# A message-passing layer on one core: fewer and differently placed loads around SyncE's queue

## The chip, the cores and the metric

The kernel runs on one core of a Trainium2 chip. The metric is the device time of one execution in microseconds (us); less is better. The median of three runs before the change is 9704.65 us (9703.06 to 9709.19).

## The reference, cut to what matters

12,500 nodes have 32 features each (8 scalars and 8 vectors of 3). 412,500 edges, sorted by receiver, have ten features (`emb`), a direction and a weight. Two small networks turn the ten features into 512 and 384 weights for each edge; with them the features of sender and receiver are multiplied, gated by a tanh, and added up at the receiver.

```python
xs, xd = x[edge_src], x[edge_dst]
s1 = concat([xs[:, :8], xd[:, :8]]); v1 = concat([xs[:, 8:].reshape(E, 8, 3), xd[:, 8:].reshape(E, 8, 3)])
w = relu(emb @ fc1_w1 / sqrt(10)) @ fc1_w2 / 4          # 512 weights of each edge
vdot1 = einsum('euk,ek->eu', v1, sh1) / SQRT3
s_t = a1 * (einsum('eu,euw->ew', s1, Wss) + einsum('eu,euw->ew', vdot1, Wvv))
v_t = a1 * (einsum('eu,euw->ew', s1, Wsv)[:, :, None] * sh1[:, None, :] + einsum('euk,euw->ewk', v1, Wvs))
# w2: 384 weights in the same way; scal, gates, vecs from s_t and v_t
edge_out = concat([tanh(scal), (vecs * tanh(gates)[:, :, None]).reshape(E, 24)]) * norm[:, None]
x = layernorm(x + segment_sum(edge_out, edge_dst, num_segments=12500))
```

## The kernel before, in words

Edges are worked on in tiles of 128 and in periods of eight tiles (1024 edges), 403 periods in all. float32 factors of matmuls are split into three bf16 pieces, which stand one below the other in six groups of rows. The work of one period is spread over five passes of a loop (`body`); in a pass each engine runs a fixed list of steps, each for the period whose turn it is. Seen from a pass `at`, the names are: `four_on`, `three_on`, `zero`, `one`, `two`, `three`, `four` for the periods at+4, at+3, at+2, at+1, at, at-1 and at-2. Between engines only semaphores set the order; each engine's list is written out by hand. Two passes stand in one turn of the loop, since buffers alternate by parity (`par`). There are passes -2 to 404; the first four and the last few stand outside the loop.

**SyncE** issues all direct loads and stores. In a pass it issues, in this order: `load_emb` for at+4 (the ten features); `load_indices` for at+3 (the senders' indices, half of a record, from `rec`); `load_late_base` for at-1 (the receivers' first node, for VectorE's window of sums); `load_near` for at+1 (for each of eight tiles it reads the tile's first receiver from `near_base` into a register and loads eight nodes' rows of `t_rows` from there); `load_near_bases` for at+3; `turn_hid(one, 0)` (a transposing DMA of `hid_parts` for layer 0, without which TensorE's `fill(one, 0)` can't start); `load_late` for `two` (the receivers' offsets, the other half of the record); `stack_emb` for at+3 (six copies of ten rows each, `emb_parts` to `emb_stack`); `stack_off`; `turn_hid(one, 1)`; and in every second pass `store_nodes` (a table piece of 256 KB to `t_rows`, and the load of `xt`).

**GpSimd** issues eight indirect gathers of node rows per pass (`gathers`, line 855), with small elementwise steps between them: `messages_scalar` needs the tanh, `hid_less_first` and `hid_less_second` make the last pieces of `hid_parts`, `emb_less_second` those of `emb_parts`.

**ScalarE** copies sums out of PSUM and applies the tanh. In a pass: `scalar_sums_back`, `emb_first`, `out_sums_out` (`osum_t`, line 1065), `node_scalars` (`prods`, line 1038), `tanh_out` (`th`, line 1070), `hidden_out`, `row_scalars`, `row_vectors`, `emb_second`, `hidden_first`, `vector_sums_out`, `near_hidden` 0, `hidden_second`, `off_hots` (eight squares), `near_hidden` 1, `scalar_sums_out`, `nodes_made`, `one_hot`, `gate_sums_out`.

**TensorE** makes each edge's weights with `fill` (line 1350, five kinds in two alternating buffers `pw`), VectorE multiplies them with the features, and TensorE adds the products by transposing them into one sum (`added`, line 1355). In a pass it ends with `nodes_made` (line 1254), `fill(one, 0)` and `gate_sums`; the next begins with `fill(two, 1)`, `out_sums`, `receivers` (line 1337, needs the receiver loads), `hidden` (line 1300, needs `emb_stack`), `four_sums_turned` (before the tanh).

**VectorE** waits for the tanh in `q_first` (`along`, line 1775), in the middle of its list; in `program` it also reads the window's first node from `late_base` into a register (line 1890).

The parts that the change touches:

Of the kernel before, what the change touches and what calls it, by code (L numbers as in the profile page):

```python
# [5 lines left out]
P = 128  # L6
G = 8
SUPER = P * G
WINDOW = 42
NEAR = 8  # L10
C = 8
F = 32
H = 16
L1, L2 = 256, 384
PIECES = 6
# [21 lines left out]
def build_gnn_layer(nc, x, src, dst, emb_t, vec, weight, fc1_w1, fc1_w2, fc2_w1, fc2_w2, out):  # L37
# [34 lines left out]

    def in_pieces(tile, dram, full, width, lo, hi, last):
# [37 lines left out]
    with ExitStack() as ctx:  # L111
# [10 lines left out]
        same_period = sb("same_period", [P, P])  # L122
# [29 lines left out]
        idx = sb("idx", [P, 2, G], I32)  # L152
        idx_dst = sb("idx_dst", [P, 2, G], I32)
        near_base = sb("near_base", [1, 2, G], I32)
# [4 lines left out]
        late_off = sb("late_off", [P, 2, G], I32)  # L159
        late_base = sb("late_base", [1, 2, G], I32)  # L160
# [28 lines left out]
        var = sb("var", [P, NB])  # L189
# [13 lines left out]

        UNIT = G * C
# [121 lines left out]
        idx_in = [sem(f"idx_in{i}") for i in range(2)]  # L326
# [10 lines left out]
        stack_in = [sem(f"stack_in{i}") for i in range(2)]  # L337
        late_in = [sem(f"late_in{i}") for i in range(2)]
        late_base_in = [sem(f"late_base_in{i}") for i in range(2)]
# [16 lines left out]
        begun = sem("begun")  # L356

# [156 lines left out]

        block = ctx.enter_context(nc.Block())
# [3 lines left out]
        def _(sp):  # L519
# [8 lines left out]
            def stack_emb(a, is_general=True):  # L528

                p = a.par  # L530
                if not is_general:
                    wait(sp, near_mm, a.before(2).n(2, 2))
                sp.wait_ge(emb_c, a.n(1, 1))
                wait(sp, hid_mm, a.before(2).n(1, 1))
# [25 lines left out]
            def load_indices(a, is_general):  # L560

                p, s, two = a.par, a.index(), a.before(2)
                wait(sp, nodes_in[p], two.k(16 * G))
                sp.dma_start(idx[:, p, :], rec[:, s, 0:G]).then_inc(idx_in[p], 16)  # L564
                if is_general:
                    wait(sp, t_edges_in, two.n(16 * G, 16 * G))
                    sp.sem_inc(begun, 1)
                    sp.dma_start(idx_dst[:, p, :], last_tiles if a.is_last() else dst_tiles[s],
                                 allow_slow_non_contiguous=True).then_inc(idx_dst_in[p], 16)

            def load_near_bases(a):
                p = a.par
                sp.dma_start(near_base[:, p, :], base_rows[:, bass.ds(a.index() * G, G)]).then_inc(near_base_in[p], 16)  # L573

            def load_near(a):
# [8 lines left out]
                for t in range(G):  # L584
                    first = nc.sync.value_load(near_base[0:1, p, t:t + 1], min_val=0, max_val=N - 1)  # L585
                    sp.dma_start(t_near[:, p, t, :], t_rows[bass.ds(first * H, NEAR * H), :]).then_inc(t_near_in[p], 16)  # L586
# [11 lines left out]
            def load_late(a, is_general):  # L598
                p, s, two = a.par, a.index(), a.before(2)
                if is_general:  # L600
                    wait(sp, rel_done, two.n(1, 1))
                    sp.dma_start(late_off[:, p, :], last_tiles if a.is_last() else dst_tiles[s],
                                 allow_slow_non_contiguous=True).then_inc(late_in[p], 16)
                else:
                    wait(sp, off_hot_done, two.n(G, G))
                    sp.dma_start(late_off[:, p, :], rec[:, s, G:2 * G]).then_inc(late_in[p], 16)  # L606
# [1374 lines left out]
```

## Time and profile before

| | us |
|---|---|
| median of the runs shown | 9704.65 |
| the profiled execution's own time | 9652.08 |
| its span, on which all rows are | 9650.3 |
| TensorE matmuls busy | 6180.1 (64%) |
| VectorE busy | 4712.0 (49%) |
| GpSimd busy | 4658.2 (48%) |
| ScalarE busy | 3364.6 (35%) |

The mean granted TensorE clock is 0.788 of full speed. SyncE has no busy time of its own in the profile; its instructions stand as SPq (the queue in which it issues). A busy share says how much an engine works, not whether the end waits for it; for that the chain of waits is read.

### The profile page before, as it was taken

Reading aid. Unit: us, or ns where it says so; the run is one execution under the profiler, and the core shown is the slowest. Engines: PE = TensorE matmul, PEld = TensorE weight load, DVE = VectorE, ACT = ScalarE, POOL = GpSimd, SP = SyncE. Lnnn points to the kernel's source line nnn. Section 1 sums busy time; section 2 is a strip of 40 time slices with the busy share of each in tenths; the row PEclk is TensorE's granted clock in tenths of the full one; section 3 lists DMA queues with packets and bytes.
Section 4 is the critical chain, followed back from the end, with each engine's and each line's share of the span. In section 5 each row is a group of like instructions: output and inputs, shape, how many; then the busy total and the mean of one; then the engine's idle time right before and its main releaser. Section 6 shows DMA issues by size and latency. Waiting matters only on the chain.

```text
span 9650.3 us, 223031 instructions
## 1 busy us (share of the span) xinstructions
PE 6180.1 (64%) x59272; PEld 5695.5 (59%) x59272; DVE 4712.0 (49%) x7823; ACT 3364.6 (35%) x10591; POOL 4658.2 (48%) x6483
## 2 busy tenths in 40 slices
PE   2566666666666666666666666666666666666666
PEld 2465665656656566565655656566565665656555
DVE  6344444444444444444444444444444444444445
ACT  2333333333333333333333333333333333333333
POOL 1545454454544545445454454545445454454543
PEclk6777787777878778777787877778777787877877
DMA  4222222222222222222222222222222222222222
GB/s 124 51 54 53 54 55 54 54 53 55 54 54 54 54 55 53 54 54 54 55 53 54 54 54 55 53 54 54 54 55 53 55 53 54 55 54 54 53 54 49
DMA packets 1898444, 535.96 MB, mean 56 GB/s; under 512 B 1783541, under 2 KB 1880551, under 8 KB 1898045
## 3 DMA queue, kind: packets, MB, share of 16 engines
q1 hardware_dynamic: 1795228, 482.38, 22.8%
q0 software_dynamic: 103168, 53.03, 3.8%
q8 instruction: 19, 0.31, 0.0%
q14 instruction: 29, 0.24, 0.0%
HBM read 203.14 MB, written 72.13 MB: 29 GB/s over the span
## 4 chain that ended last, share of the span: by engine, by line
SPq 76%; issue 19%; PE 2%; DVE 1%; DMA 1%; POOL 1%; ACT 0%; POOLq 0%; DVEq 0%; ACTq 0%
SPq L536 19%; SPq L585 15%; SPq L586 14%; SPq L556 10%; SPq L526 4%; SPq L606 2%; SPq L564 2%; SPq L544 2%; SPq L596 2%; SPq L573 2%; SPq L592 1%; SPq L612 1%; PE p L1355 1%; SPq L446 1%; DVE prods L1626 1%
## 5 line engine op out<-in xcount | busy, mean ns | idle before, releaser
L855 POOL DMA_INDIRECT nodes<-x_rows,idx x3224 | 3094.8, 960 | 732.9 <-issue 673.5
L1350 PE MATMUL pw<-w_stack,work 128*128 128x128 bf16 x16120 | 1466.6, 244 | 3032.0 <-DMA work<-hid_parts 2998.4
L1355 PE MATMUL p<-identity,prods 128*128 128x128 f32 x20956 | 3177.5, 314 | 0.6 <-ACT gates_t L1060 0.5
L1350 PEld LDWEIGHTS pw<-w_stack,work 128*128 128x128 bf16 x16120 | 1174.0, 110 | 3390.5 <-issue 3095.3
L1355 PEld LDWEIGHTS p<-identity,prods 128*128 128x128 f32 x20956 | 2886.8, 168 | 1.8 <-issue 1.7
L1689 DVE TENSOR_TENSOR prods<-pw,V 128x1024 f32<-128x1024 f32 x403 | 493.6, 1225 | 2813.4 <-PE pw L1350 2813.4
L832 POOL TENSOR_TENSOR emb_rest<-emb,emb_parts 80x128 f32<-80x128 f32 x403 | 171.6, 426 | 3232.5 <-ACT emb_parts L971 3225.7
L1060 ACT ACTIVATE gates_t<-p 128x128 f32<-128x128 f32 x403 | 111.7, 277 | 4285.8 <-PE p L1355 4285.8
L1775 DVE TENSOR_TENSOR along<-p,r_all 128x192 f32<-128x192 f32 x403 | 144.2, 358 | 1726.2 <-ACT th L1070 1726.2
L1733 DVE TENSOR_TENSOR prods<-pw,M 128x1024 f32<-128x1024 f32 x806 | 976.9, 1212 | 1.6 <-PE pw L1350 1.6
L1337 PE MATMUL pz<-work 128*128 128x64 f32 x6448 | 767.9, 272 | 10.3 <-DMA work<-t_rows 10.0
L1337 PEld LDWEIGHTS pz<-work 128*128 128x128 f32 x6448 | 755.0, 193 | 10.7 <-issue 10.2
L1077 ACT ACTIVATE spare<-node_iota,late_off 128x42 f32<-128x42 f32 x3224 | 747.7, 314 | 0.0
L1741 DVE TENSOR_TENSOR prods<-pw,VT 128x1536 f32<-128x1536 f32 x403 | 705.0, 1749 | 0.5 <-PE pw L1350 0.5
L806 POOL TENSOR_TENSOR msg<-th,w_all 128x128 f32<-128x128 f32 x403 | 164.2, 408 | 755.4 <-ACT th L1070 755.4
L1020 ACT ACTIVATE work<-pa 128x512 f32<-128x512 f32 x806 | 468.2, 581 | 0.8 <-PE pa L1313 0.7
L1706 DVE TENSOR_TENSOR prods<-pw,S 128x512 f32<-128x512 f32 x403 | 278.8, 692 | 269.5 <-PE pw L1350 266.0
L1007 ACT ACTIVATE hid_parts<-hid 128x768 bf16<-128x768 f32 x403 | 336.4, 835 | 0.0
L1434 PE MATMUL p<-spare,msg 128*32 128x42 f32 x6448 | 322.0, 203 | 1.7 <-DVE msg L1785 1.7
L1065 ACT ACTIVATE osum_t<-p 128x256 f32<-128x256 f32 x403 | 154.4, 383 | 474.9 <-PE p L1355 455.0
L1313 PE MATMUL pa<-emb_stack,w_near 96*128 96x512 bf16 x806 | 308.0, 382 | 1.8 <-ACT work L1020 1.3
L1038 ACT ACTIVATE prods<-pz 128x64 f32<-128x64 f32 x403 | 114.4, 284 | 557.9 <-PE pz L1337 557.9
(174 smaller groups left out, 8232.2 us busy)
## 6 DMA issues: line engine op xcount, KB each, us to landing
work<-t_rows SPq DMA_DIRECT2D x3224, 32.0 KB
t_rows<-t_stage SPq DMA_DIRECT2D x205, 256.0 KB
nodes<-x_rows,idx POOLq DMA_INDIRECT x3224
emb_stack<-emb_parts SPq DMA_DIRECT2D x2418, 20.0 KB
emb<-in_emb_t SPq DMA_DIRECT2D x403, 40.0 KB
work<-hid_parts SPq DMA_TRANSPOSE x806, 2.9
idx<-rec SPq DMA_DIRECT2D x403, 4.0 KB, 1.7
near_base<-base_rows SPq DMA_DIRECT2D x403, 0.0 KB
```

The source lines that it names most:

```text
L536: sp.dma_start(emb_stack[K1 * g:K1 * g + K1, p, :].rearrange("k (c e) -> k c e", c=G), emb_parts[:, p, part, :]).then_inc(stack_in[p], 16)
L556: sp.dma_start_transpose(hid_t[:, layer, p, :, :], hid_parts[:, p, layer * G:layer * G + G, :].rearrange("e t k -> e (t k)")).then_inc(tur ...
L585: first = nc.sync.value_load(near_base[0:1, p, t:t + 1], min_val=0, max_val=N - 1)
L586: sp.dma_start(t_near[:, p, t, :], t_rows[bass.ds(first * H, NEAR * H), :]).then_inc(t_near_in[p], 16)
L855: nc.gpsimd.indirect_dma_start(nodes[:, p, t, :], None, x_rows, bass.IndirectOffsetOnAxis(ap=idx[:, p, t:t + 1], axis=0)).then_inc(nodes_i ...
L1077: nc.scalar.activation(off_hot[:, t, :], node_iota[:, :], ACT.Square, bias=off[:, t:t + 1]).then_inc(off_hot_done, 1)
L1337: mm = nc.tensor.matmul(z[:, :, t, :], hid_near[:, P * t:P * t + P], t_near[:, a.par, t, :].rearrange("p (c w) -> p c w", w=C), start=(t = ...
L1350: mm = nc.tensor.matmul(pw[:, slot, t, :], hid_t[:, layer, a.par, t, :], w2_stack[:, lo:lo + W], start=True, stop=True)
L1355: return nc.tensor.matmul(out, column, identity[:, :], start=first, stop=last, is_transpose=True)
L1689: nc.vector.tensor_tensor(prod_v01.rearrange("p u k t w -> p k t u w"), weights(0, ring, 0).unsqueeze(1).broadcast_to([P, 2, G, C, C]), V[ ...
L1733: nc.vector.tensor_tensor(prod_g[:, :, half, :, :].rearrange("p u t w -> p t u w"), weights(2 + half, ring), M[:, a.par, :, :].unsqueeze(3 ...
L1741: nc.vector.tensor_tensor(prod_o[:, :, 0:3, :, :].rearrange("p u k t w -> p k t u w"), weights(4, ring, 1).unsqueeze(1).broadcast_to([P, 3 ...
```

## The change

- `stack_emb` is split. `store_emb`, for at+3, stores the three pieces of the ten features to a new tensor `emb3` in memory; one pass later `stack_emb`, now for at+2, loads the six groups of rows from there in three loads (three pieces, two pieces, one piece), after a wait for the store. ScalarE's `emb_first` waits for the store in place of the copies.
- One load of four neighbouring records (`load_records`, tile `near`) takes the place of `load_indices` and `load_late`: GpSimd reads indices from its last record and ScalarE offsets from its first. It waits for the gathers of the pass before.
- One load of four periods' bases (`load_bases`) takes the place of `load_near_bases` and `load_late_base`. It waits until VectorE and ScalarE have read the buffer (`window_begun`, `windows_begun`).
- SyncE's `load_near` issues the loads of tiles 0 to 3; ScalarE issues those of tiles 4 to 7 in a new `load_near` between `out_sums_out` and `node_scalars`. Both read four indices with one call.
- `same_period` and `var` lose buffers of their own and lie in `gates_t` and `vs_t`.

```diff
+    emb3 = nc.dram_tensor("emb3", [2, 3, K1, SUPER], BF16, kind="Internal").ap()
...
+        def load_windows(eng, p, t0):
+            half = G // 2
+            _, firsts = nc.values_load_multi_w_load_instructions(
+                near_base[0:1, p, 3 * G + t0:3 * G + t0 + half], engines=[eng.engine], min_val=0, max_val=N - 1)
+            for t in range(half):
+                eng.dma_start(t_near[:, p, t0 + t, :], t_rows[bass.ds(firsts[t] * H, NEAR * H), :]
+                              ).then_inc(t_near_in[p], 16)
...
+            def store_emb(a):
+                p = a.par
+                sp.wait_ge(emb_c, a.n(1, 1))
+                sp.sem_inc(begun, 1)
+                wait(sp, stack_in[p], a.before(2).k(16 * 3))
+                sp.dma_start(emb3[p].rearrange("a k (c e) -> (k c) a e", c=G), emb_parts[:, p, :, :]).then_inc(emb_stored[p], 16)
+
+            def stack_emb(a, is_general):
                 p = a.par
+                sp.wait_ge(emb_stored[p], a.k(16))
+                sp.sem_inc(begun, 1)
+                if is_general:
+                    wait(sp, hid_mm, a.before(2).n(1, 1))
+                else:
                     wait(sp, near_mm, a.before(2).n(2, 2))
-                for g, part in enumerate((0, 1, 2, 0, 1, 0)):
-                    sp.dma_start(emb_stack[K1 * g:K1 * g + K1, p, :].rearrange("k (c e) -> k c e", c=G),
-                                 emb_parts[:, p, part, :]).then_inc(stack_in[p], 16)
+                first = 0
+                for parts in (3, 2, 1):
+                    sp.dma_start(emb_stack[K1 * first:K1 * (first + parts), p, :],
+                                 emb3[p, 0:parts].rearrange("a k e -> (a k) e")).then_inc(stack_in[p], 16)
+                    first += parts
...
+            def load_records(at, i, is_general):
+                p = at.par
+                lo, hi = (0, 4) if i is None else (max(0, -i), min(4, NS - i))
+                if lo >= hi:
+                    return
+                if i is None or 0 <= i + 1 < NS:
+                    sp.wait_ge(nodes_in[1 - p], At(at.b, at.d + 1).k(16 * G))
+                    sp.sem_inc(begun, 1)
+                if not is_general:
+                    wait(sp, off_hot_done, at.before(2).n(G, G))
+                    sp.sem_inc(begun, 1)
+                sp.dma_start(near[:, p, lo:hi, :], rec[:, bass.ds(at.index() + lo, hi - lo), :]).then_inc(near_in[p], 16)
...
+            def load_bases(at, i):
+                p = at.par
...
+                wait(sp, window_begun, at.n(1, -2))
+                sp.sem_inc(begun, 1)
+                wait(sp, windows_begun, at.n(1, 1) if i is None else min(i + 1, NS))
+                sp.sem_inc(begun, 1)
+                sp.dma_start(near_base[:, p, G * lo:G * hi],
+                             base_rows[:, bass.ds((at.index() + (lo - 1)) * G, (hi - lo) * G)]).then_inc(near_base_in[p], 16)
...
+                    if zero is not None:
+                        stack_emb(zero, is_general)
+                        if not is_general:
+                            stack_off(zero)
                     if four_on is not None:
                         load_emb(four_on)
+                    load_records(at, i, is_general)
                     if one is not None and not is_general:
                         load_near(one)
+                    if not is_general:
+                        load_bases(at, i)
                     if one is not None and i != -1:
                         turn_hid(one, 0)
                     if three_on is not None:
+                        store_emb(three_on)
                     if one is not None and i != -1:
                         turn_hid(one, 1)
...
+            def load_near(a):                                   # ScalarE
+                p = a.par
+                act.wait_ge(near_base_in[p], a.k(16))
+                act.sem_inc(begun, 1)
+                wait(act, d_mm, a.before(2).n(1, 1))
+                act.sem_inc(begun, 1)
+                wait(act, t_stored, a.before(1).k(16, 16 * (LEAD - 1)))
+                act.sem_inc(begun, 1)
+                load_windows(nc.scalar, p, G // 2)
+                act.sem_inc(windows_begun, 1)
...
                     if four is not None:
                         out_sums_out(four)
+                    if one is not None and fast:
+                        load_near(one)
                     if two is not None:
                         node_scalars(two)
```

## Rows read from the trace of the kernel before

**Rows 1.** The page: chain that ended last, by engine, by line.

```profile
SPq 76%; issue 19%; PE 2%; DVE 1%; DMA 1%; POOL 1%; ACT 0%; POOLq 0%; DVEq 0%; ACTq 0%
SPq L536 19%; SPq L585 15%; SPq L586 14%; SPq L556 10%; SPq L526 4%; SPq L606 2%; SPq L564 2%; SPq L544 2%; SPq L596 2%; SPq L573 2%; SPq L592 1%; SPq L612 1%; PE p L1355 1%; SPq L446 1%; DVE prods L1626 1%
```

**Rows 2.** Waits, whole span: engine, line <- releaser: total us, times, longest.

```profile
PE pw L1350 <- DMA work<-hid_parts: 2998.4, 401, 9.5
```

**Rows 3.** The page: DMA queues: packets, MB, share of 16 engines.

```profile
q1 hardware_dynamic: 1795228, 482.38, 22.8%
```

**Rows 4.** Timeline of SyncE, one pass: start us, us, instructions.

```profile
5007.03 0.59 SPq L592 DMA_DIRECT2D t_rows<-t_stage  x1
...
5009.27 0.90 SPq L526 DMA_DIRECT2D emb<-in_emb_t  x1
5010.48 0.36 SPq L564 DMA_DIRECT2D idx<-rec  x1
5011.21 0.26 SPq L612 DMA_DIRECT2D late_base<-base_rows  x1
5012.87 8.29 SPq L586 DMA_DIRECT2D work<-t_rows  x8
5021.35 0.30 SPq L573 DMA_DIRECT2D near_base<-base_rows  x1
5021.99 1.32 SPq L556 DMA_TRANSPOSE work<-hid_parts  x1
...
5024.18 4.94 SPq L536 DMA_DIRECT2D emb_stack<-emb_parts  x6
5029.41 0.32 SPq L544 DMA_DIRECT2D emb_stack<-off_rows_of  x1
5030.00 1.27 SPq L556 DMA_TRANSPOSE work<-hid_parts  x1
5031.47 0.88 SPq L526 DMA_DIRECT2D emb<-in_emb_t  x1
```

**Rows 5.** Timeline of SyncE at the start: a ten-row weight load from memory.

```profile
3.91 0.40 SPq L634 DMA_DIRECT2D w<-in_fc_w  x1
```

**Rows 6.** Register reads, lines 585 and 1890: duration ns min/median/max.

```profile
L585 SPq TENSOR_LOAD <-near_base x8: 264/268/465, 5011.9 to 5020.1; - x8
...
L1890 DVEq TENSOR_LOAD <-late_base x2: 303/306/309, 5013.0 to 5036.9; - x2
```

**Rows 7.** Timelines of ScalarE and TensorE: an ordinary and a late pass.

```profile
5034.07 0.28 ACT L1070 ACTIVATE th<-p 128x128 f32<-128x128 f32 x1 [0.49 <-PE p L1429]
...
5039.91 0.38 PE L1254 MATMUL pa<-wt,xt 48*64 48x256 bf16 x2 [0.48 <-ACT work L1020]
...
9578.42 0.40 PE L1254 MATMUL pa<-wt,xt 48*64 48x256 bf16 x2
...
9583.58 0.38 ACT L1065 ACTIVATE osum_t<-p 128x256 f32<-128x256 f32 x1 [1.53 <-PE p L1355]
...
9585.65 0.28 ACT L1070 ACTIVATE th<-p 128x128 f32<-128x128 f32 x1
```

**Rows 8.** TensorE's gate sums; stretches: us, busy (count) by engine, granted clock.

```profile
5025.78 3.32 PE L1355 MATMUL p<-identity,prods 128*128 128x128 f32 x16
...
9579.21 1.92 PE L1355 MATMUL p<-identity,prods 128*128 128x128 f32 x16
...
5017.00:5018.00 1.00, 0.00 (x0) 0.00 (x0) 0.99 (x4) 0.22 (x1) 0.69 (x2) 1.00 0.17 40
5025.00:5026.00 1.00, 1.00 (x10) 1.00 (x10) 0.00 (x0) 0.00 (x0) 0.00 (x0) 0.50 0.09 21
...
9580.00:9585.00 5.00, 5.00 (x52) 4.99 (x51) 4.57 (x10) 0.88 (x3) 0.00 (x0) 1.00 0.30 58
```

**Rows 9.** GpSimd's last gather of a pass; landing of the transposes.

```profile
5043.31 0.98 POOL L855 DMA_INDIRECT nodes<-x_rows,idx  x1 [0.16 <-issue]
...
DMA to landing us min/median/max: 2.7/2.9/9.3
```

More of the change, by code:

```diff
@@ L324, in build_gnn_layer @@
         acc_zero = sem("acc_zero")
-        idx_in = [sem(f"idx_in{i}") for i in range(2)]
+        near_in = [sem(f"near_in{i}") for i in range(2)]
         idx_dst_in = [sem(f"idx_dst_in{i}") for i in range(2)]
@@ L337, in build_gnn_layer @@
         stack_in = [sem(f"stack_in{i}") for i in range(2)]
+        emb_stored = [sem(f"emb_stored{i}") for i in range(2)]
         late_in = [sem(f"late_in{i}") for i in range(2)]
-        late_base_in = [sem(f"late_base_in{i}") for i in range(2)]
         nodes_in = [sem(f"nodes_in{i}") for i in range(2)]
@@ L575, in load_near, with load_destinations @@
+            def load_destinations(a):
+                p, s, two = a.par, a.index(), a.before(2)
+                wait(sp, t_edges_in, two.n(16 * G, 16 * G))
+                sp.sem_inc(begun, 1)
+                sp.dma_start(idx_dst[:, p, :], last_tiles if a.is_last() else dst_tiles[s],
+                             allow_slow_non_contiguous=True).then_inc(idx_dst_in[p], 16)
             def load_near(a):
@@ L583, in load_near @@
                 sp.sem_inc(begun, 1)
-                for t in range(G):
-                    first = nc.sync.value_load(near_base[0:1, p, t:t + 1], min_val=0, max_val=N - 1)
-                    sp.dma_start(t_near[:, p, t, :], t_rows[bass.ds(first * H, NEAR * H), :]).then_inc(t_near_in[p], 16)
+                load_windows(nc.sync, p, 0)
             def store_nodes(a):
@@ L704, in _ @@
                         load_first_chunk(m + 2)
[L706 removed]
+            store_emb(At(0, 0))
             sp.wait_ge(s_general, 1)
@@ L711, in body @@
                 def body(at, i):
+                    three_on, four_on = stage(at, 3, i), stage(at, 4, i)
+                    zero, one, two = (stage(at, by, i) for by in (2, 1, 0))
                     if i == -2:
-                        load_indices(At(0, 0), is_general)
-                        if not is_general:
-                            load_near_bases(At(0, 0))
-                            stack_off(At(0, 0))
+                        load_first_record()
+                        if is_general:
+                            load_destinations(At(0, 0))
                     if i == -1:
@@ L856, in gathers @@
                         nodes[:, p, t, :], None, x_rows,
-                        bass.IndirectOffsetOnAxis(ap=idx[:, p, t:t + 1], axis=0)
+                        bass.IndirectOffsetOnAxis(ap=near[:, 1 - p, 3, t:t + 1], axis=0)
                     ).then_inc(nodes_in[p], 16)
@@ L969, in emb_first @@
                 act.wait_ge(emb_in[p], a.k(16))
-                wait(act, stack_in[p], a.before(2).k(16 * PIECES))
+                wait(act, emb_stored[p], a.before(2).k(16))
                 nc.scalar.activation(emb_parts[:, p, 0, :], emb[:, p, :], ACT.Copy).then_inc(emb_a, 1)
@@ L1887, in body @@
                     if four is not None and not is_general:
-                        dve.wait_ge(late_base_in[four.par], four.k(16))
+                        dve.wait_ge(near_base_in[1 - four.par], four.k(16, 32 if four.par else 16))
                         dve.sem_inc(begun, 1)
-                        first = nc.vector.value_load(late_base[0:1, four.par, 0:1], min_val=0, max_val=N - 1)
+                        first = nc.vector.value_load(near_base[0:1, 1 - four.par, 0:1], min_val=0, max_val=N - 1)
+                        dve.sem_inc(window_begun, 1)
                     if three is not None:
```

82 lines of the change are left out of this document (27 added, 55 removed).

## The prediction, made before the change was run

> **What bounds the kernel now.** I read the page's chain of work first, because it says what the end waited for. The reader is to see there that SyncE's own queue (SPq) holds 76% of the span and that no wait of it is named: the six piece loads of line 536 take 19%, the register reads and loads of lines 585 and 586 take 29%, the transposes of line 556 take 10% [rows 1]. So the period is the time SyncE needs to issue its list. The waits say the same from the other end: TensorE stands 2998.4 us in 401 waits, 7.5 us a period, for the transposed `hid_parts` that SyncE issues [rows 2]. The transfers don't bound: SyncE's queue keeps the 16 DMA engines 22.8% busy [rows 3]. Then SyncE's timeline: one pass (5009.27 to 5031.47) takes 22.20 us; with the store of every second pass, 2.24 us from its start to the next `emb` load, the mean is about 23.2 [rows 4]. That mean times 401 is 9300 of the span of 9650.3; the rest is set-up and tail, which the change hardly touches.
>
> **SyncE's new pass.** Steps are taken from start to start, so gaps are in them [rows 4].
> - Kept: `emb` load 1.21; `stack_off` 0.59; the transposes 1.5 and 1.47; the store and its `xt` load 2.24 in every second pass, 1.12 a pass. Sum 5.9.
> - Pieces, 5.2 us now for six copies between SBUF and SBUF. They become one store of 80 rows of three pieces and three loads of 30, 20 and 10 whole rows. A copy of whole ten-row weights out of memory was issued in 0.40 us at the start [rows 5], a ten-row SBUF copy takes some 0.8. I take 0.45 for each load with 0.25 for two waits, so 1.6 (bounds 1.2 and 2.7), and 1.1 for the store with its waits (bounds 0.6, a simple load with its wait, and 2.7, three of today's piece copies). It is nearest to the simple ones.
> - Records: two loads become one, 0.73 for a load like `idx`, and 0.2 for a wait: 0.9 (0.8 to 1.1). Bases: two become one, 0.64 and two waits: 0.85 (0.7 to 1.0).
> - Receiver loads: eight take 8.48 us, 1.06 each. Four remain: 4.24 if nothing else changes. But four indices are read by one call; if that is one read of 0.268 us [rows 6] in place of four, 0.9 goes: 3.35. I take 3.8, between, and 1.1 for the waits before (the 1.66 between `late_base` and the first load, less a load).
> The sum is 5.9+1.6+1.1+0.9+0.85+3.8+1.1 = 15.3 us a pass; the low ends give 13.5, the high ends 19.
>
> **What is late next: the loop through the tanh.** With 15.3 for SyncE, TensorE no longer stands 7.5 us, and the other engines' loop decides. It can be read where the transposes came early, in the last passes. I count from the start of the tanh `th`. In an ordinary pass the matmul of line 1254 starts 5.84 later (5034.07 to 5039.91); in the last pass in which nothing is late, `osum_t` starts 5.16 after that matmul and the next `th` 7.23 after it (9578.42, 9583.58, 9585.65) [rows 7]. With 0.3 for the hidden matmuls absent there, the loop is 5.84+7.23+0.3 = 13.35 us, and `osum_t` comes at +11.0. This holds at the full level of TensorE's clock (granted 1.00, 2.4 GHz, from 9580 to 9585). After the wait for the transpose, in which TensorE idled nearly 9 us, it is granted 0.50 (1.2 GHz), and the sixteen sums take 3.32 us instead of 1.92 [rows 8]. In the first us or two without work the grant still holds, so I take the shorter waits to come as warm.
>
> **ScalarE's four loads lie in that loop.** `load_near` stands between `out_sums_out` and `node_scalars`, and `tanh_out` is behind both. VectorE's `along` waits for `th`, and so does the message on GpSimd; hidden_out, the row copies and both `near_hidden` are queued behind it. No load issued by ScalarE is in the trace. By SyncE's four it is 4.24 and some waits; another engine's queue reads a register somewhat slower (VectorE's 0.306 against 0.268 [rows 6]). I take 0.4 for three waits, 0.3 for the read, four times 0.9: 4.3 us (bounds 2.5, if the queue runs ahead and issue is cheap, and 5.6). Some 1.7 of it replace a wait that was there, from `osum_t` to `prods`. `th` then starts at 11.0+4.3+0.2 = 15.5 us: the tanh loop grows from 13.35 to 15.5, 2.1 us lost by the change and hidden before only because SyncE was later. The new semaphore waits of ScalarE are mostly passed: the bases come a pass ahead. The one near its edge is `t_stored`, wanted at about +11 in every second pass, when a store issued at about +8 needs some 3 to land; I give it 0.3 a period.
>
> **A loop over two periods, through GpSimd and SyncE.** `load_records` now waits for the eight gathers of the pass before, and everything else of SyncE's pass is queued behind it: receiver loads, bases, transposes, the store. The last gather starts 9.24 after `th` (5043.31) and, if it lands like a transpose, 2.9 later: +12.1 [rows 9]. Then records 0.9, receiver loads 4.9, bases 0.85, so the transpose starts at +18.8 and lands at +21.7. From the fill it releases to `osum_t` are 4.8, and 4.5 to the next `th`: 31.0 for two periods, 15.5 each.
>
> **Sum.** Three bounds meet: 15.3, 15.5 and 15.5. With 0.3 for the store and 0.3 for near misses between chains this close, I expect 16.1 us a period against 23.17. 401 x 7.07 = 2835 us; 9650.3 - 2835 = 6815 of span. The profiled execution took 1.8 more than its span (9652.08), and the median of the runs shown stands 52.6 above that; with both, 6870 us. Shorter set-up (fewer loads before the loop) and the two tensors that now share buffers are worth nothing I can measure: they lie outside the 401 periods.
>
> **A rule against it.** The profile first: SyncE's issue holds the chain at 76% while its transfers fill 22.8% of the DMA engines [rows 1, 3]. The Trainium skill, "DMA: Bandwidth & Descriptors", "Issuing engines are not separate DMA queues", says that DMAs of several engines run on the same 16 DMA engines and that a second issuer saves only the sequencer's time, which is usually small beside the DMA. By that "usually", the four moved loads bring nothing, and the period falls only by SyncE's other savings, to about 19.5, some 8200 us; by the rows it is just this time that bounds. The rule is a reason to leave some chance there.
>
> **Rivals.**
> A. SyncE stays the bound: the store of 240 pieces or the loads of 30, 20 and 10 rows cost as much as today's copies. For: a ten-row copy does cost 0.8 now. Against: the ten-row load from memory took 0.40. Period 16.8 to 19.5, middle 18: 9650 - 401x5.2 = 7570, with the 54 about 7620. The rule's case lies at its upper end and is in its chance.
> B. The clock falls in the new waits before `th`. For: cold after 9 us of idling. Against: the new waits are 1 to 3 us in a piece. Cold sums and fill add 1.6: period 17.7, about 7510.
> C. ScalarE issues in less than 3 us and the read is shared: period 14.4, near the 13.35 of the bare loop: about 6190.
> D. Not faster, by one mechanism: the piece store in memory. SyncE waits for its landing at the head of the next pass, with all of its list behind it. Two steps (1.47 and on average 1.12) cover 2.6 us and the store's issue. Every us beyond is a us of the period. It decides from a landing of 10.5 us on (15.3 + 7.9 = 23.2); with 11.1 the period is 23.8 and the time about 9950. For: a transpose once took 9.3 to land [rows 9]. Against: its median is 2.9.
> E. No change in time: the same chain, wherever SyncE's list is cut, is fed by a fixed transfer. Against it stands all of rows 1.
>
> **Chances.** Forecast (15.3 to 16.8, own range 6550 to 7150) 0.46; A 0.20; B 0.13; C 0.17; D 0.03; E 0.01. Faster by over 0.2% (what a measurement of this kernel can tell) 0.96, within 0.01, slower 0.03. The range reaches to the middle of C, 6200, and into A's upper half, 7750.
>
> **What would show it.** After the change SyncE's queue no longer holds most of the chain; ScalarE's queue appears in it with the four loads; SyncE shows waits at `load_records`. The piece loads take under 0.5 us each. TensorE's wait for `hid_parts` falls from 7.5 us a period to under 2, its clock is near full, and from `osum_t` to `th` there are 4 to 5 us in place of 2.1. Period 16.1. Wrong would be: SPq still above 60% of the chain (A), clock under 0.9 (B), under 3 us from `osum_t` to `th` (C), a long wait of SyncE on `emb_stored` (D).

## The result and the profile after

| | before | after |
|---|---|---|
| median, us | 9706.92 (9703.06 to 9711.13, 4 runs) | 7672.35 (7621.77 to 7688.22, 4 runs) |
| ratio after to before | | 0.7895, 95% interval 0.7856 to 0.7934 |
| profiled execution, us (span) | 9652.08 (9650.3) | 7688.22 (7686.4) |
| mean granted TensorE clock | 0.788 | 0.922 |
| period, from `th` to `th`, us | 23.17 | 18.28 |

Faster, inside the stated range (6200 to 7750) by 78 us, and 800 us above the forecast time (6870). It lies outside the forecast's own range (6550 to 7150): the time falls in the room that was left for rival A.

The page of the changed kernel, queues and chain; they answer to [rows 3] and [rows 1]. SyncE's queue has gone from 76% of the chain to 1%. TensorE is at its head, ScalarE's queue has 12% with the new loads (lines 521 and 524), and 10% is something that the profile can't name.

```profile
q1 hardware_dynamic: 1428533, 464.10, 26.7%
...
q10 hardware_dynamic: 232128, 52.93, 3.1%
...
PE 45%; issue 18%; ACTq 12%; another core or an unknown queue 10%; DVE 6%; ACT 6%; DVEq 1%; SPq 1%; POOL 1%; DMA 0%; POOLq 0%
PE p L1404 24%; PE pw L1399 8%; ACTq L524 7%; ACTq L521 4%; PE p L1483 3%; PE pz L1386 3%; DVE prods L1762 3%; PE pa L1303 2%; ACT spare L1112 1%; PE pa L1362 1%; ACT th L1105 1%; ACT spare L1119 1%; DVE prods L1675 1%; PE pz L1427 1%
```

Waits of the changed kernel, whole span (engine, line <- releaser: total us, times, longest); the last row answers to [rows 2]. TensorE's wait for the transposed `hid_parts` fell from 2998.4 us to 4.0. In its place `gates_t` waits 1357.3 us for a releaser called "remote". This program has one core, so there is no remote one. "Remote" here is a step of a semaphore (the count by which one engine tells another that an instruction is done) for which the profile found no instruction that ended at that moment.

```profile
DVE along L1824 <- ACT th L1105: 2147.0, 396, 8.2
POOL msg L841 <- ACT th L1105: 1369.4, 396, 10.9
ACT gates_t L1095 <- remote: 1357.3, 363, 5.2
...
DVE prods L1755 <- remote: 437.2, 336, 1.7
...
PE pw L1399 <- DMA work<-hid_parts: 4.0, 4, 3.2
```

SyncE's own waits (the same columns). It waits 3.2 us a pass (1275.4 over 401) for the pieces it is to store, and hardly at `load_records` (35.6), so its issues alone no longer set the period.

```profile
SPq L544 <- POOL emb_parts L872: 1275.4, 363, 12.6
...
SPq L592 <- DMA nodes<-x_rows,near: 35.6, 31, 4.3
```

What "remote" is shows in one pass. Timelines of TensorE, ScalarE and SyncE (start us, us, what; in brackets the idle time before and its releaser), then stretches of that pass (us, busy and count of PE, PEld, DVE, ACT, POOL, then the granted clock, DMA share and GB/s):

```profile
4004.76 1.92 PE L1404 MATMUL p<-identity,prods 128*128 128x128 f32 x16
4006.51 0.61 PE L1399 MATMUL pw<-w_stack,work 128*128 128x128 bf16 x8
4006.96 0.39 PE L1445 MATMUL pz<-halves,st_t 128*128 128x64 f32 x2
4010.55 3.68 PE L1404 MATMUL p<-identity,prods 128*128 128x128 f32 x16 [3.21 <-ACT gates_t L1095]
```

```profile
4004.41 0.59 ACT L1060 ACTIVATE t_stage<-pa 64x512 f32<-64x512 f32 x1 [0.40 <-PE pa L1303]
4004.90 0.47 ACT L1119 ACTIVATE spare<-spare 128x336 f32<-128x336 f32 x1
4010.22 0.28 ACT L1095 ACTIVATE gates_t<-p 128x128 f32<-128x128 f32 x1 [4.85 <-remote]
...
4014.26 0.38 ACT L1100 ACTIVATE osum_t<-p 128x256 f32<-128x256 f32 x1 [3.00 <-PE p L1404]
4016.04 1.91 ACTq L524 DMA_DIRECT2D work<-t_rows  x4
4018.20 0.28 ACT L1073 ACTIVATE prods<-pz 128x64 f32<-128x64 f32 x1 [3.55 <-PE pz L1386]
4018.73 0.28 ACT L1105 ACTIVATE th<-p 128x128 f32<-128x128 f32 x1 [0.25 <-PE p L1478]
```

```profile
4006.90 0.01 SPq L641 DMA_DIRECT2D xt<-x  x1
```

```profile
4006.00:4010.00 4.00, 1.34 (x17) 1.20 (x14) 2.66 (x5) 0.00 (x0) 2.82 (x4) 0.91 0.56 113
4010.00:4011.00 1.00, 0.45 (x2) 0.45 (x3) 0.69 (x1) 0.49 (x3) 0.00 (x0) 0.50 0.17 28
```

The sixteen gate sums end at 4006.68. `gates_t` waits for nothing that ends later, and starts 3.5 us later, at 4010.22; TensorE, which needs `gates_t`, stands 3.2 us. After that the grant is 0.50, and the next sixteen sums take 3.68 us instead of 1.92 [rows 8]. An issue of SyncE in that stretch is recorded with 0.01 us; in e11 below the same one takes 0.69. That is no single case. SyncE's receiver loads of the changed kernel (view of line 524; ns min/median/max):

```profile
L524 SPq DMA_DIRECT2D work<-t_rows x1612: 3/333/1535, 275.4 to 7609.0; - x180
```

In e13 below, where no step is late, they take 332 to 705 ns, none less.

I worked this out for every pass: from the end of each matmul that steps a semaphore to the time at which the trace records the step. A step that comes over 0.4 us late I call late.

| step of TensorE, after | passes late | mean of the late ones, us |
|---|---|---|
| gate sums (L1404) | 99% | 2.62 |
| `fill(two, 1)` (L1399) | 99% | 3.07 |
| scalar sums turned (L1445) | 96% | 2.89 |
| window sums (L1483) | 94% | 0.86 |

In the kernel before each of these is 0%. The steps of VectorE, ScalarE and GpSimd that the traces record are on time in both. But the changed kernel's trace records only 65% of VectorE's steps and 67% of ScalarE's (the kernel before: over 96% of each); the shares above, too, are of recorded steps.

### The profile page after: what moved, and what is told of

It is laid out like the page before. It is cut to its first block, busy times and chain, and to the rows that moved or that the text cites. A ratio compares the mean times of both kernels' runs of the same rounds, so it can differ in the third digit from the quotient of the medians.

```text
span 7686.4 us, 221061 instructions
## 1 busy us (share of the span) xinstructions
PE 5908.3 (77%) x59272; PEld 5330.7 (69%) x59272; DVE 4694.7 (61%) x7823; ACT 3294.6 (43%) x10591; POOL 4659.5 (61%) x6483
## 3 DMA queue, kind: packets, MB, share of 16 engines
q0 software_dynamic: 103168, 53.03, 4.8%
## 4 chain that ended last, share of the span: by engine, by line
PE 45%; issue 18%; ACTq 12%; another core or an unknown queue 10%; DVE 6%; ACT 6%; DVEq 1%; SPq 1%; POOL 1%; DMA 0%; POOLq 0%
PE p L1404 24%; PE pw L1399 8%; ACTq L524 7%; ACTq L521 4%; PE p L1483 3%; PE pz L1386 3%; DVE prods L1762 3%; PE pa L1303 2%; ACT spare L1112 1%; PE pa L1362 1%; ACT th L1105 1%; ACT spare L1119 1%; DVE prods L1675 1%; PE pz L1427 1%
## 5 line engine op out<-in xcount | busy, mean ns | idle before, releaser
L890 POOL DMA_INDIRECT nodes<-x_rows,near x3224 | 3095.7, 960 | 733.6 <-issue 679.8
L1404 PE MATMUL p<-identity,prods 128*128 128x128 f32 x20956 | 2825.8, 290 | 892.5 <-issue 485.2
L1404 PEld LDWEIGHTS p<-identity,prods 128*128 128x128 f32 x20956 | 2483.9, 150 | 947.3 <-issue 688.9
L1399 PE MATMUL pw<-w_stack,work 128*128 128x128 bf16 x16120 | 1286.1, 224 | 361.7 <-DVE prods L1762 312.9
L1399 PEld LDWEIGHTS pw<-w_stack,work 128*128 128x128 bf16 x16120 | 1018.2, 100 | 666.8 <-DVE prods L1762 407.1
L1386 PE MATMUL pz<-work 128*128 128x64 f32 x6448 | 894.8, 300 | 14.3 <-ACT M L1089 11.0
L1386 PEld LDWEIGHTS pz<-work 128*128 128x128 f32 x6448 | 885.8, 220 | 26.8 <-issue 12.5
L1112 ACT ACTIVATE spare<-node_iota,near 128x42 f32<-128x42 f32 x3224 | 748.5, 316 | 0.0
L1095 ACT ACTIVATE gates_t<-p 128x128 f32<-128x128 f32 x403 | 111.6, 277 | 1457.4 <-remote 1357.3
L1060 ACT ACTIVATE t_stage<-pa 64x512 f32<-64x512 f32 x403 | 238.2, 591 | 293.6 <-PE pa L1303 162.6
```

What stands on the lines that cost most here:

```text
L890: nc.gpsimd.indirect_dma_start(nodes[:, p, t, :], None, x_rows, bass.IndirectOffsetOnAxis(ap=near[:, 1 - p, 3, t:t + 1], axis=0)).then_inc ...
L1112: nc.scalar.activation(off_hot[:, t, :], node_iota[:, :], ACT.Square, bias=off[:, t:t + 1]).then_inc(off_hot_done, 1)
L1386: mm = nc.tensor.matmul(z[:, :, t, :], hid_near[:, P * t:P * t + P], t_near[:, a.par, t, :].rearrange("p (c w) -> p c w", w=C), start=(t = ...
L1399: mm = nc.tensor.matmul(pw[:, slot, t, :], hid_t[:, layer, a.par, t, :], w2_stack[:, lo:lo + W], start=True, stop=True)
L1404: return nc.tensor.matmul(out, column, identity[:, :], start=first, stop=last, is_transpose=True)
```

## The experiments

The period is the mean from one start of `th` to the next, "remote" the wait of `gates_t` so named, in us over the span. Ratios are to the kernel before, measured beside each run (9653 us beside e10 to e13, 9704 to 9707 beside the others).

| kernel | median us | ratio (95%) | clock | period | remote |
|---|---|---|---|---|---|
| after | 7672 | 0.7895 (0.7856 to 0.7934) | 0.922 | 18.28 | 1357 |
| e1 six SBUF copies again | 8521 | 0.8785 (0.8767 to 0.8804) | 0.848 | 20.33 | 1753 |
| e3 all eight loads on SyncE | 7807 | 0.8051 (0.8012 to 0.8090) | 0.873 | 18.54 | 1088 |
| e5 pieces stored twice | 8193 | 0.8444 (0.8427 to 0.8462) | 0.892 | 19.51 | 1626 |
| e6 ScalarE's loads split | 7503 | 0.7719 (0.7700 to 0.7739) | 0.924 | 17.86 | 1414 |
| e2 before, pieces through memory | 8535 | 0.8792 (0.8766 to 0.8817) | 0.826 | 20.38 | 23 |
| e7 gathers 0 to 3 alone | 6618 | 0.6817 (0.6798 to 0.6837) | 0.986 | 15.61 | 0 |
| e8 second transpose a plain copy | 8230 | 0.8477 (0.8391 to 0.8564) | 0.877 | 19.53 | 1536 |
| e9 before, half of the loads | 7957 | 0.8196 (0.8172 to 0.8220) | 0.857 | 18.93 | 132 |
| e10 gathers 4 to 7 alone | 6473 | 0.6711 (0.6698 to 0.6724) | 0.978 | 15.16 | 0 |
| e11 e6 and gathers 2, 3 early | 6338 | 0.6565 (0.6554 to 0.6576) | 0.978 | 14.91 | 0 |
| e12 gathers 2, 3 behind the steps | 6558 | 0.6793 (0.6782 to 0.6805) | 0.978 | 15.44 | 0 |
| e13 gathers 2, 3 early | 6467 | 0.6705 (0.6694 to 0.6716) | 0.978 | 15.19 | 0 |

Two theories stood first. S: the new piece store, 80 rows of three short pieces, holds the signals up. G: GpSimd's gathers do, where they run beside a working TensorE.

**e1, the piece store undone.**

```diff
-                        store_emb(three_on)
+                        stack_pieces(three_on, is_general)   # six copies SBUF to SBUF, as before
```

> The changed kernel, with the ten features' pieces again in six copies from SBUF to SBUF (the store to memory and its three loads are gone); all else as changed. In the changed trace the signals of TensorE's matmuls arrive up to 5 us late, most of all some 4 us after the piece store was issued. Theory S (the piece store in memory holds up TensorE's signals): the late signals go, from t_stage to gates_t falls from 4.6 us to 2.5, and the period is then SyncE's list: 15.1 of work + 5.2 for six copies - 2.9 for the store, loads and waits = 17.4, so 7350 us. Rival G (the gathers and the table store, which now run beside a working TensorE, hold them up, whoever moves the pieces): from t_stage to gates_t stays at 4 us or more, SyncE's longer list comes on top, period 18.5 to 19.5, 7750 to 8150 us.

8520.61 us, slower by 848, and the gate sums are late in 99% of the passes by 3.75 us on average. Without any piece store the hold-ups are longer, so S falls as the cause. It overshot G's number (7750 to 8150) as well: with the six copies the hold-ups are longer, which G didn't have.

**e3, ScalarE's loads given back.**

```diff
                 load_windows(nc.sync, p, 0)
+                load_windows(nc.sync, p, G // 2)
```

> The changed kernel with all eight receiver loads on SyncE (two reads of four indices), none on ScalarE. From osum_t to prods falls from 3.85 to 1.73 us again. If SyncE's issue bounds (15.1 of work + 4 loads of 0.54 and a second read with four address steps, 1.3): 18.6 us a pass plus what the late signals add, period 18.6 to 19.5, 7800 to 8150 us. If the page's word holds that a second issuer saves only little: no difference, 7670 us. If ScalarE's loads in the tanh loop cost more than they save (their 2.1 us lost in full): period 16.5 to 17, below 7300 us.

7807.42 us: of 2035 us gained, the moved loads are worth 135, in a kernel whose signals are late. SyncE's queue is 30% of the chain there, TensorE 31%, and the gate sums are late in 75% of the passes.

**e5, the piece store doubled.**

```diff
+                sp.dma_start(emb3b[p]..., emb_parts[:, p, :, :]).then_inc(emb_stored[p], 16)
```

> The changed kernel with the pieces stored twice, to two tensors in memory; the loads wait for both. SyncE pays 0.4 us more, inside the 3.1 us that it waits in each pass. Theory S (the piece store holds up TensorE's signals): the hold-ups grow with the number of pieces, by 0.6 to 1.5 us a period, 7900 to 8300 us, and the time between t_stage and gates_t grows. Rival G (gathers and table store): no change within 1%, 7600 to 7750 us.

8192.84 us, in S's range, though e1 speaks against S. The store is not the cause, but the second one lengthens the hold-ups ("remote" 1626 against 1357). SyncE's queue has 103,168 packets more (1,531,701), 256 a period. In e1 it has 76,167 more, and is slower too. Yet the number of packets is not the measure: e8 has 367,536 fewer, with the same bytes, and is slower as well.

**e6, two of ScalarE's loads ahead of `osum_t`, two behind.**

```diff
                     if one is not None and fast:
-                        load_near(one)
+                        load_near(one, True)    # tiles 4, 5
+                    if four is not None:
+                        out_sums_out(four)
+                    if one is not None and fast:
+                        load_near(one, False)   # tiles 6, 7
```

> The changed kernel with ScalarE's four receiver loads parted: two before osum_t is copied, in the 1.8 us in which ScalarE waits for the out sums anyway, two after it, where it waits 1.7 us for prods. If the tanh loop is what bounds a pass, the 2.1 us that the four loads add between osum_t and prods go nearly all: period 16.3 to 16.8, 6850 to 7100 us. If late signals or SyncE bound instead, the gain is below 0.5 us a period, 7480 us or more.

7503.10 us, at the end where late signals bind. From `gates_t` to `osum_t` it took 3.90 us (after: 2.87), from `osum_t` to `prods` 2.35 (3.85).

**e2, the kernel before with the pieces through memory and nothing else.**

> The kernel before with one part of the change alone: the pieces through memory (one store, three loads a pass). SyncE's list falls by 2.9 us (5.2 for six copies against some 1.2 for the loads, 0.6 for the waits and 0.5 for the store): if issue alone bounds, period 20.3 against 23.17, 8530 us. Theory S is already in doubt from the copies run; if it held, TensorE's signals would be late here too. Theory G (late signals wherever TensorE works while GpSimd issues gathers 4 to 7 and the next one): TensorE still idles some 4 us a pass, so part of its signals come late but are hidden by SyncE: same 8530.

8534.95 us, on the expected value: while SyncE still binds, this part alone gives 1172 us. Window sums are late in 99% of the passes and vector sums in 77%; the wait for SyncE hides them.

**e7, gathers 4 to 7 left out.**

```diff
-                for t in tiles:
+                for t in [t for t in tiles if t < 4]:
```

> The changed kernel with gathers 4 to 7 of each pass left out (the node rows of these tiles are zeros). Theory G (these gathers, which now run beside TensorE's fill and gate sums, hold up the signals): the gate sums' signal, 2.6 us late in 99 of 100 passes of the changed kernel, comes in time; from t_stage to gates_t falls from 4.6 to 2.5 us; period 15.2 to 16.2, 6450 to 6850 us. Rival D (SyncE's own descriptors: transpose, table store and loads from memory in one stretch): late signals stay, from t_stage to gates_t stays above 3.5, period 17 to 18, 7150 to 7550 us.

6618.34 us, as G had it. The gate sums are on time in every pass, and the clock is 0.986. Only the window sums are still late, by 0.66 us.

**e8, the second transposing DMA replaced.** It writes `hid_t` untransposed.

```diff
+                if layer:
+                    sp.dma_start(hid_t[:, layer, p, :, :], hid_parts[:, p, layer * G:layer * G + G, :])...
```

> The changed kernel with the second layer's transposing DMA replaced by a plain copy of the same bytes (the second layer's weights are then made from unturned data). If it is the transpose that holds up the signals together with the gathers: late signals mostly gone, period 16 to 16.6, 6800 to 7050 us. Theory G without it: signals late as before, period 17.8 to 18.3, 7500 to 7700 us.

8229.66 us, outside both ranges; gate sums late in 99% of the passes by 3.23 us. The second transposing DMA is not the cause; the first is still there. Why it is 557 us slower than the changed kernel stays open.

**e9, the kernel before with the receiver loads of tiles 0 to 3.** No part of the change is in it; tiles 4 to 7 use the rows of 0 to 3.

> The kernel before with the receiver loads of tiles 4 to 7 left out (TensorE takes tiles 0 to 3 twice); no part of the change is in it. SyncE's list falls by 4.2 us. If issue alone bounds: period 18.9, 7950 us. Theory G: as TensorE now idles only some 3 us, its next fill and gate sums come beside gathers 5 to 7, and their signals are late here too, in over half of the passes, with none of the changed parts; period 18.9 to 19.8, 7950 to 8320 us. If a part of the change causes the late signals: none late here.

7956.89 us, on the value of an issue-bound SyncE. Late signals appear here as well: window sums in 97% of the passes, vector sums in 74%, gate sums in 38% (G had over half). So none of the new operations is needed for them; the kernel before, which has none, gets them once SyncE has less to issue.

**e10, gathers 0 to 3 left out.** The mirror of e7.

```diff
-                for t in tiles:
+                for t in [t for t in tiles if t >= 4]:
```

> The changed kernel without gathers 0 to 3 of each pass; 4 to 7 stay at their places, beside the end of TensorE's list (the node rows of tiles 0 to 3 are zero). GpSimd's list and the number of gathers are as short as where gathers 4 to 7 were left out (6618 us). Theory 'gathers beside TensorE': what counts is the stretch in which they run, so the signals of the gate sums stay late in at least some of the passes: 6900 to 7500 us. Rival 'number': it was the shorter list of GpSimd, or half of the small packets, that gave the time back, wherever they stood: 6550 to 6750 us.

6472.98 us: the rival's side, and below its range (6550 to 6750). Four gathers run beside TensorE's last sums, and no signal of any line is late. G as stated falls.

**e11, e6 with gathers 2 and 3 ahead of GpSimd's wait for the tanh.** All eight gathers are there.

```diff
+                    if zero is not None:
+                        gathers(zero, (2, 3))
                     if four is not None:
                         messages_scalar(four, windows, more)
                     if zero is not None:
-                        gathers(zero, (2,))
                         hid_less_first(zero)
-                        gathers(zero, (3,))
```

> The kernel with ScalarE's loads split (7503 us), and gathers 2 and 3 issued before GpSimd waits for the tanh, where it idles 2.7 to 3.7 us a pass; four gathers in place of six then follow each other after the tanh. Theory 'gathers beside TensorE': hold-ups of TensorE's signals begin later or end earlier, by about the time of two gathers (2.6 us of the 2.6 us mean): 6600 to 7200 us. Rival 'number': the same gathers and packets, only moved, so within 1% of 7503 us; and if the two gathers delay the messages, up to 7700 us.

6338.38 us, 15.5% below e6 (6338 over 7503; 15.0% by the ratios) for two instructions moved within one list. No signal is late. Both theories missed: the one gave at least 6600, the other about 7503.

**e12 and e13: place or count.** Both are the changed kernel with gathers 2 and 3 moved. e13 has them early, as e11. e12 has them later than they were:

```diff
                     if zero is not None:
-                        gathers(zero, (2,))
                         hid_less_first(zero)
-                        gathers(zero, (3,))
                     if three_on is not None:
                         emb_less_second(three_on)
                     if zero is not None:
+                        gathers(zero, (2,))
+                        hid_less_second(zero)
+                        gathers(zero, (3,))
                         gathers(zero, (4,))
-                        hid_less_second(zero)
                         gathers(zero, (5,))
```

> The changed kernel (7672 us) with gathers 2 and 3 moved behind emb_less_second: after the tanh GpSimd does messages, hid_less_first and emb_less_second with no gather between, then seven gathers, with hid_less_second after the first of them. Where the two gathers were issued before the tanh, no signal was late. Theory 'place': what held the signals up was gathers between the small steps, 1 to 5 us after the tanh, so none is late here either: 6450 to 6700 us. Theory 'count after the tanh': seven gathers still start after the tanh and run beside TensorE, now later, so signals of the gate sums stay late: 7400 to 8000 us.

> The changed kernel with gathers 2 and 3 ahead of the wait for the tanh and nothing else. No signal should be late. Against the same with ScalarE's loads split (6338 us, period 14.91) all four loads stand again between osum_t and prods: 3.8 us there instead of 2.25, and 2.45 from gates_t to osum_t instead of 3.6. If the tanh loop binds, as the prediction had it, the period is 0.4 us longer: 6450 to 6550 us. If GpSimd's list or TensorE binds by now, the place of the loads does not matter: 6330 to 6380 us.

e12: 6558.20 us, no late signal, though seven gathers start after the tanh. So it is not their count after the tanh but their place. e13: 6467.09 us, none late. GpSimd's list in the changed kernel, one pass after the tanh:

```profile
3998.28 0.41 POOL L841 TENSOR_TENSOR msg<-th,w_all 128x128 f32<-128x128 f32 x1 [4.90 <-ACT th L1105]
3998.93 0.98 POOL L890 DMA_INDIRECT nodes<-x_rows,near  x1 [0.23 <-issue]
3999.93 0.68 POOL L879 TENSOR_TENSOR hid_rest<-hid,hid_parts 128x256 f32<-128x256 f32 x1
4000.77 0.96 POOL L890 DMA_INDIRECT nodes<-x_rows,near  x1 [0.16 <-issue]
4001.75 0.43 POOL L872 TENSOR_TENSOR emb_parts<-emb_rest,emb_parts 80x128 bf16<-80x128 f32 x1
4002.34 0.96 POOL L890 DMA_INDIRECT nodes<-x_rows,near  x1 [0.16 <-issue]
4003.32 0.68 POOL L884 TENSOR_TENSOR hid_parts<-hid_rest,hid_parts 128x256 bf16<-128x256 f32 x1
4004.16 0.96 POOL L890 DMA_INDIRECT nodes<-x_rows,near  x1 [0.16 <-issue]
4005.42 0.94 POOL L890 DMA_INDIRECT nodes<-x_rows,near  x1 [0.30 <-issue]
```

and in e12:

```profile
4007.51 0.41 POOL L841 TENSOR_TENSOR msg<-th,w_all 128x128 f32<-128x128 f32 x1 [1.06 <-ACT th L1105]
4009.09 0.67 POOL L879 TENSOR_TENSOR hid_rest<-hid,hid_parts 128x256 f32<-128x256 f32 x1 [1.17 <-ACT hid_parts L1042]
4009.73 0.42 POOL L872 TENSOR_TENSOR emb_parts<-emb_rest,emb_parts 80x128 bf16<-80x128 f32 x1
4010.30 0.98 POOL L890 DMA_INDIRECT nodes<-x_rows,near  x1 [0.15 <-issue]
4011.30 0.75 POOL L884 TENSOR_TENSOR hid_parts<-hid_rest,hid_parts 128x256 bf16<-128x256 f32 x1
4012.21 0.95 POOL L890 DMA_INDIRECT nodes<-x_rows,near  x1 [0.16 <-issue]
4013.47 0.94 POOL L890 DMA_INDIRECT nodes<-x_rows,near  x1 [0.30 <-issue]
```

The same gathers at the same spacing (1.3 to 1.9 us); in e12 they begin 2.8 us after the message, not 0.65. TensorE and ScalarE then, in e13 (timelines as above): the sums run without a pause, each sixteen in 1.92 us, and `gates_t` starts 0.03 us after its sums end (13.91 and 1.92 make 4015.83).

```profile
4013.91 1.92 PE L1404 MATMUL p<-identity,prods 128*128 128x128 f32 x16
4015.68 0.62 PE L1399 MATMUL pw<-w_stack,work 128*128 128x128 bf16 x8
4016.14 0.39 PE L1445 MATMUL pz<-halves,st_t 128*128 128x64 f32 x2
4016.36 1.92 PE L1404 MATMUL p<-identity,prods 128*128 128x128 f32 x16
```

```profile
4015.86 0.28 ACT L1095 ACTIVATE gates_t<-p 128x128 f32<-128x128 f32 x1 [1.34 <-PE p L1404]
4018.31 0.38 ACT L1100 ACTIVATE osum_t<-p 128x256 f32<-128x256 f32 x1 [1.11 <-PE p L1404]
4020.09 1.88 ACTq L524 DMA_DIRECT2D work<-t_rows  x4
4022.22 0.28 ACT L1073 ACTIVATE prods<-pz 128x64 f32<-128x64 f32 x1 [3.52 <-issue]
4022.34 0.27 ACT L1105 ACTIVATE th<-p 128x128 f32<-128x128 f32 x1
```

**What is shown and what stays open.** Shown: two gathers at their place among GpSimd's small steps cost the changed kernel 1205 us (7672 to 6467, e13; by the two ratios to the kernel before, 1155), and TensorE's late signals go with them. Not shown is why. In the changed kernel the held gate sums end 0.8 to 0.9 us after the start of a gather, and the held steps of `fill(two, 1)` and of the scalar sums come mostly 1.6 to 2.0 us after the start of the last gather before them. But that a gather is under way is not enough: in every second pass of e11 the gate sums end 1.2 us after the start of one and are on time. Nor is the place enough: the kernel before has the gathers at the same times after the tanh and no late signal, and e2 and e9, whose GpSimd list is the same, have them. Place, a SyncE ahead with its list, and traffic all bear on it. Which unit of the chip they meet in no run here tells.

One rival is untested: the recording of the profile itself. Every time on record comes with a recorded span and clock, so none is of an execution without the recorder. Counted over the steps of TensorE, VectorE, ScalarE and GpSimd, 25% are missing in the changed kernel's trace and 16 to 31% in e1, e2, e3 and e5 to e9. In the kernel before and in e10 to e13 it is 2 to 4%. So the kernels that have late steps are exactly those that lose many records, and SyncE's issues of 3 ns belong to them too. Whatever holds the steps up may hold up the records as well, or the recording may be what holds them up. Whether an execution without the recorder would lose these 1205 us isn't shown.

## Why the prediction was right, and where it was 800 us off

Means of the tanh loop, us per period, from starts on ScalarE (the predicted column is the prediction's sum, cut at the same points; its 0.6 for the store and near misses is not in a segment):

| | predicted | after | e13 |
|---|---|---|---|
| `th` to `t_stage` | 6.25 | 6.76 | 6.24 |
| `t_stage` to `gates_t` | 2.3 | 4.60 | 2.55 |
| `gates_t` to `osum_t` | 2.4 | 2.87 | 2.43 |
| `osum_t` to `prods` | 4.3 | 3.85 | 3.83 |
| `prods` to `th` | 0.2 | 0.18 | 0.12 |
| sum | 15.5 | 18.28 | 15.19 |

- *SyncE's pass, 15.3 us*: 1.7 too high. In the changed kernel 18.28 less the 3.2 it waits at `store_emb` is 15.1, and less its smaller waits 14.8. With the signals on time the period less all of SyncE's waits is 13.6 (15.19 less 1.6 in e13; the same in e10, e11 and e12), at the sum of the low ends (13.65; the prediction has 13.5, and 19 where its high ends add up to 18.7). Inside it, a piece load took 0.33 us (0.45 foreseen) and the store 0.35. SyncE's four receiver loads are 0.33 each plus one `TENSOR_LOAD` of 0.50 and register work.
- *Rival A, SyncE stays bound*: wrong as a mechanism (SPq 1% of the chain), though its time, 7620, is near the result. The right number for the wrong reason. *C* is out as well: from `osum_t` to `th` there are 4.0 us, not under 3. *D*: SyncE's waits for the piece store come to 1.3 us in the whole span.
- *ScalarE's four loads, 4.3 us (2.5 to 5.6)*: 3.85. They cost 0.34 us each, with 0.31 for the read and 0.15 four times for register work:

```profile
L521 ACTq FUSED_REGOPS  x1612: 147/147/162, 262.3 to 7606.1; - x180
...
L521 ACTq TENSOR_LOAD <-near_base x403: 304/308/326, 262.0 to 7605.1; - x135
```

```profile
L524 ACTq DMA_DIRECT2D work<-t_rows x1612: 339/341/1786, 263.4 to 7609.5; - x180
```

- (The rows are of the views of lines 521 and 524, ns min/median/max.) That the loads lie in the loop is shown by e11 against e13: splitting them gives 129 us (6467 to 6338), 0.28 us a period where I expected 0.4.
- *The two-period loop through `load_records`, 15.5*: not the bound; SyncE waits there 35.6 us in all. At 18.28 nothing depends on it. It shows in e12, whose gathers are later: SyncE waits at `load_records` in all 403 passes (643.3 us), at a period of 15.44. In e13 no single list binds at 15.19; its chain (page, by engine) goes through SyncE's queue, TensorE, DMA and ScalarE's queue side by side, though SyncE's own list would fit in 13.6:

```profile
SPq 26%; issue 22%; PE 19%; DMA 10%; ACTq 9%; DVE 7%; ACT 3%; DVEq 3%; POOL 1%; POOLq 0%
```

- *The tanh loop, "read where the transposes came early, in the last passes"*: this is the step that failed. It took 5.16 us from the matmul of line 1254 to `osum_t` from those passes [rows 7]. No gather runs in them, since there are no more periods to gather for, so they could not show that signals come late beside gathers. The last gather of the kernel before, 19 us ahead of the matmul at 9578.42 that the loop was read from:

```profile
9559.15 0.98 POOL L855 DMA_INDIRECT nodes<-x_rows,idx  x1 [0.16 <-issue]
```

  Measured: 2.3 us more from `t_stage` to `gates_t`. No rival had it.
- *Rival B, the clock*: it did fall, but as a consequence. I had written that "in the first us or two without work the grant still holds"; the pause here was 3.2 us and the grant was 0.50 after it. The difference of 0.4 us from `gates_t` to `osum_t` fits this (the sums after the pause took 3.68 us), and in e13, without the pause, it is gone. Of the 0.5 from `th` to `t_stage` some 0.3 is again a late signal: the step of the matmul of line 1303, which `t_stage` needs, is late in 15% of the passes by 2.0 us.
- The size: 18.28 - 15.19 = 3.09 us a period, times 401 is 1239 us, against 1205 between the medians of after and e13. With signals on time the kernel takes 6467 us, 403 below the forecast. Its sum of 15.5 was 0.3 too high, and its 0.6 for the store and near misses did not come. So the 800 us are 1205 of a cost not foreseen, less 403 by which the forecast was too high. That the result still lies in the stated range is luck: the mechanism foreseen gives 6467, and what lifted the time to 7672 was in none of the prediction's terms.
- *The rule against the change*: e3 against after puts 135 us, 1.7%, on the second issuer. By this number the case agrees with the Trainium skill ("DMA: Bandwidth & Descriptors", "Issuing engines are not separate DMA queues"), which calls what a second issuer saves usually small. It does not agree with the time of 8200 that I derived from it, since SyncE's other savings gave more: e3 has them alone and takes 7807. And the 135 us hold where late signals bind. With signals on time the second issuer should be worth more: SyncE's list is 3.3 us longer in e3 than in the changed kernel (18.1 against 14.8), and 13.6 + 3.3 = 16.9 is 1.7 above the period of e13, some 680 us in 401 periods. That is an estimate; no run has all eight loads on SyncE and the signals on time.

## What to carry to other kernels

When the bound is taken away, the loop that is next has to be read in passes that hold all the other traffic; the last passes of a loop are the cleanest and lack exactly what collides. Look for waits whose releaser the profile can't name: compare the end of the matmul with the start of the one that waits for it, and if there are microseconds between, move the transfers about before doing anything to the arithmetic. If the trace also lacks many records, try, where you can, whether the wait is there without the recorder. Here the order within an engine that was not on the path (GpSimd, 61% busy) was worth 1205 us, over half of what the whole change gave, and cost nothing; put the gathers behind the small steps (e12) or in the time in which their engine waits anyway (e13).

## What was not expected of the hardware

- In these recorded executions a semaphore step of TensorE's can arrive on average 2.6 to 3.7 us after the matmul that makes it ended (gate sums of the changed kernel and of e1), in 99% of the passes. No recorded step of VectorE, ScalarE or GpSimd does. Nothing is wrong in the page's busy shares then; TensorE is 77% busy in the changed kernel and 85% in e11.
- Added transfers can lengthen these hold-ups: one more store of 256 packets a period cost 520 us (e5 against after), six SBUF copies in place of a store and three loads 848 (e1).
- Issuing a row of whole-row loads takes 0.33 us each; the copies between SBUF and SBUF that they replaced take 0.8 [rows 4].
- Reading four registers by one call costs one `TENSOR_LOAD` (0.31 us on ScalarE, 0.50 on SyncE) and 0.15 us of register work for each value. The register work was there before as well; on SyncE the call saves 0.57 us of four reads of 0.268 [rows 6].
